# Paged-attention layer stack on one core: which bytes the values' trip through memory carries, and the order of stores, gathers and expert loads around it

## What is computed

```
x = x + einsum('bct,bcd->bdt', x, W0[cond])                        # layer 0: a 32x32 mix per sequence
x = x + x @ W^T + s * (x @ A[id]^T) @ Bm[id]^T                     # layer 1: dense plus a low-rank adapter
x = x + attention(x)                                               # layer 2
x = x + x @ W3[expert_id] + b3[expert_id]                          # layer 3: one 256x256 expert per sequence
```

## Time and profile before

| | us |
|---|---|
| median of 3 runs (155.38 to 156.30) | 156.03 |
| the profiled execution's own time | 154.9 |
| its span | 153.1 |
| busy: PE, DVE, ACT, POOL | 117.3, 88.8, 85.8, 62.0 |

### The profile page before, as it was taken

How to read it: one execution, slowest core, us unless ns; L and a number is a source line. 1 busy time by engine, 2 the same in 40 slices (tenths; PEclk the granted TensorE clock), 3 DMA queues, 4 the chain that set the end, 5 groups by cost and what they waited for, 6 DMA issues and landing times.

```text
span 153.1 us, 4138 instructions
## 1 busy us (share of the span) xinstructions
PE 117.3 (77%) x1418; PEld 91.0 (59%) x1418; DVE 88.8 (58%) x315; ACT 85.8 (56%) x236; POOL 62.0 (41%) x65
## 2 busy tenths in 40 slices
PE   7569599999989586076598392892599999999762
PEld 7559458998374163074466272672387787776631
DVE  0597988857528824860344003610867999989361
ACT  3119634698743629256589721472438878888200
POOL 7666779000008764787233300330333444734000
PEclk9999999999999977659969758699569999999999
DMA  3982999999963444799739998999976676766110
GB/s 94 244 249 62 370 424 407 423 405 374 395 173 100 132 119 114 247 313 392 315 110 269 422 355 210 401 377 279 253 232 205 197 242 204 222 207 180 37 39 34
DMA packets 29100, 37.60 MB, mean 246 GB/s; under 512 B 9497, under 2 KB 26781, under 8 KB 27438
## 3 DMA queue, kind: packets, MB, share of 16 engines
q1 hardware_dynamic: 26136, 23.98, 50.0%
q0 software_dynamic: 2528, 12.82, 22.2%
q10 hardware_dynamic: 416, 0.56, 1.2%
HBM read 31.39 MB, written 10.04 MB: 271 GB/s over the span
## 4 chain that ended last, share of the span: by engine, by line
DMA 42%; PE 20%; SPq 17%; issue 9%; POOL 5%; DVE 3%; ACT 2%; POOLq 1%; DVEq 0%
DMA kv_rows<-blkp 15%; DMA wr_rows<-blkp 11%; PE bank L1117 5%; DMA blkp<-wr_rows,patch_i 4%; PE bank L1063 4%; POOL wr_rows L500 4%; DMA blkp<-in_L_cond_W 4%; PE bank L1075 3%; PE bank L1128 3%; SPq L386 3%; DMA mask_rows<-span_m 3%; DMA scal<-in_L_cond_scalings 3%; SPq L364 2%; SPq L365 2%; SPq L348 2%
## 5 line engine op out<-in xcount | busy, mean ns | idle before, releaser
L520 POOL TENSOR_TENSOR xin_m<-xin_m,ri 128x704 f32<-128x704 f32 x15 | 21.8, 1454 | 44.4 <-DVE ri L924 44.4
L674 ACT ACTIVATE xin_m<-kvn_m,nb 128x176 f32<-128x176 f32 x64 | 27.6, 443 | 9.2 <-DVE nb L911 9.2
L911 DVE CUSTOM_DVE_ANT_0 kvn_m<-bank,mask_m 128x176 f32<-128x176 f32 x64 | 18.0, 336 | 14.6 <-PE bank L1063 11.0
L951 DVE TENSOR_TENSOR blkp<-blkp,cst 128x512 f32<-128x512 f32 x16 | 15.6, 1015 | 17.6 <-DMA blkp<-in_L_cond_W 17.6
L1063 PE MATMUL bank<-kt_m,natQ 32*64 32x176 f32 x256 | 15.7, 366 | 10.0 <-DVE nb L911 9.1
L1063 PEld LDWEIGHTS bank<-kt_m,natQ 32*64 32x64 f32 x256 | 9.5, 150 | 14.2 <-issue 13.1
L500 POOL DMA_INDIRECT wr_rows<-kvn_m,row_i x8 | 8.8, 1104 | 21.3 <-DMA wr_rows<-blkp 19.1
L684 ACT COPY x_m<-bank 128x512 f32<-128x512 f32 x16 | 9.4, 590 | 13.0 <-PE bank L1075 12.8
L1043 PE MATMUL bank<-cst,blkp 121*128 121x121 f32 (+1 forms) x48 | 9.0, 352 | 7.8 <-DMA blkp<-wr_rows,patch_i 7.8
L1043 PEld LDWEIGHTS bank<-cst,blkp 121*128 121x128 f32 (+1 forms) x48 | 7.3, 190 | 10.0 <-DMA blkp<-wr_rows,patch_i 9.0
L674 ACT ACTIVATION_READ_ACCUMULATOR xin_m<-kvn_m,nb 128x1 f32 x64 | 12.8, 200 | 0.0
(11 more groups left out here) (194 smaller groups left out, 257.4 us busy)
## 6 DMA issues: line engine op xcount, KB each, us to landing
blkp<-in_L_cond_W SPq DMA_DIRECT2D x32, 256.0 KB, 3.5
kv_rows<-blkp SPq DMA_DIRECT2D x3, 2048.0 KB, 10.3
wr_rows<-blkp SPq DMA_DIRECT2D x1, 1536.0 KB, 16.5
mask_m<-mask_rows SPq DMA_DIRECT2D x32, 44.0 KB, 5.4
vm_m<-kv_rows SPq DMA_DIRECT2D x4, 320.0 KB, 4.4
xin_m<-in_x SPq DMA_DIRECT2D x2, 512.0 KB, 5.6
out<-wq_m SPq DMA_DIRECT2D x8, 128.0 KB, 3.5
vm_m<-kv_rows SPq DMA_DIRECT2D x2, 384.0 KB, 4.6
```

Of the source, the lines that this page charges most:

```text
L520: pool.tensor_tensor(e_, e_, ri[:, p % 2, :].unsqueeze(2).broadcast_to([P, 4, KEYS]), ALU.mult).then_inc(s_pn, 1)
L674: act.activation(pr_seq(n % 2, u, j), S[:, n % 2, u, j, :], ACT.Exp, bias=nb[:, n % 2, 2 * u + j:2 * u + j + 1], scale=-1.0, accum_out=rs[ ...
L911: dve.tensor_tensor_reduce(S[:, n % 2, u, j, :], bank[2 + (2 * n + u) % 3][:, j * KEYS:(j + 1) * KEYS], mask[:, 2 * n + j, :], -SCALE, 3e3 ...
L951: tt(w_, w_, ident.unsqueeze(1).broadcast_to([P, B4, P]), ALU.add).then_inc(s_wx, 1)
```

## The change

1. SP: the 8 mask reads ahead of `wr_rows` out now come behind it. Masks 0 to 15 are read there; 16 to 19 behind values out 0, 20 to 23 behind values out 1, 24 to 31 behind values out 2. The loop waits for masks in groups of eight.
2. Values out sends only the v numbers and only the unit's own partitions (121, 121, 110 rows of 16 pieces of 512 bytes) to `v_rows`; the way back reads these.
3. SP's order is values out 0, back 0, experts 0 to 3, out 1, back 1, experts 4 to 7, out 2, back 2, experts 8 to 15. The latter now lie in `blkp[1]`.
4. POOL: patch 2 waits for values out 0. The bias gathers go into the pair loop, one a step at p = 2 to 9.
5. The copies (1,0), (1,1) and (2,1) go from ScalarE to VectorE, behind rotations(0).
6. q_part 2 and 3, but for their sums, go into the loop (n = 0 to 5), and turn_k 4 to 11 as well (two a step at n = 0 to 3; before, 4 and 5 lay ahead of the loop). ScalarE's zeroing of the v tails comes before x2 copies 2 and 3.

```diff
@@ -113,7 +114,7 @@
     with ctx:
         wr_rows = nc.dram_tensor("wr_rows", [ROWS, 2 * KV], F32).ap()
         wr_blocks = wr_rows.rearrange("(p o) c -> p (o c)", o=BLOCK)
-        kv_rows = nc.dram_tensor("kv_rows", [NU, P, BLOCK * 2 * KV], F32).ap()
+        v_rows = nc.dram_tensor("v_rows", [NU, P, BLOCK, KV], F32).ap()
         mask_rows = nc.dram_tensor("mask_rows", [P, KEYS + LAST], BF16).ap()
         cst = sb("cst", [P, cols.width])
...
@@ -196,8 +197,8 @@
         blkp = [sb(f"blkp{u}", [P, CH]) for u in range(NU)]
         by_o = [t[:, :].rearrange("p (o k c) -> p o k c", o=BLOCK, k=2) for t in blkp]
         blkw = blkp[2]
-        We = lambda b: blkp[(0, 2)[b % NE // 8]][:, (b % 8) * KC * D:(b % 8 + 1) * KC * D].rearrange("p (c o) -> p c o", c=KC)
-        We4 = lambda g: blkp[(0, 2)[g % B4 // 2]][:, g % 2 * B4 * KC * D:(g % 2 + 1) * B4 * KC * D] \
+        We = lambda b: blkp[b % NE // 8][:, (b % 8) * KC * D:(b % 8 + 1) * KC * D].rearrange("p (c o) -> p c o", c=KC)
+        We4 = lambda g: blkp[g % B4 // 2][:, g % 2 * B4 * KC * D:(g % 2 + 1) * B4 * KC * D] \
             .rearrange("p (b c o) -> p b c o", b=B4, c=KC)
         kt_m = sb("kt_m", [P, B * KEYS])
...
@@ -313,13 +315,16 @@
                 raw[i][0:n, :].rearrange("p (g o d) -> p g o d", g=G, o=BLOCK)
         MIX_DVE, MIX_ACT = ((0, 0), (0, 1), (0, 2), (1, 0), (1, 1)), ((0, 3), (1, 2), (1, 3))
-        KT_BANK = (3, 4, 0, 7, 3, 4, 7, 0, 7, 0, 7, 7)
-        KT_FREE = (0, 0, 0, 0, 1, 2, 4, 3, 7, 8, 9, 11)
+
+        KT_BANK = (3, 4, 0, 7, 0, 7, 0, 7, 7, 7, 7, 7)
+        KT_FREE = (0, 0, 0, 0, 3, 4, 5, 6, 8, 9, 10, 11)
         Q_BANK = (1, 2, 1, 2)
         QT_BANK = (5, 6)
-        QT_STEP = {1: 4, 2: 5, 3: 6, 4: 7}
-        KT_STEP = {0: (6, 7), 1: (8, 9), 2: (10,), 3: (11,)}
+        QT_STEP = {3: 4, 4: 5, 6: 6, 7: 7}
+        KT_STEP = {0: (4, 5), 1: (6, 7), 2: (8, 9), 3: (10, 11)}
+        Q_STEP = {0: (2, 1), 1: (2, 2), 2: (2, 3), 3: (3, 1), 4: (3, 2), 5: (3, 3)}
+        BIAS_STEP = 2
         L1_BANK = (5, 6)
...
@@ -362,15 +367,13 @@
             def load_mask(b):
                 x = sp.value_load(shift_i[0:1, b:b + 1], min_val=0, max_val=LAST)
-                sp.dma_start(mask[:, b, :], mask_rows[:, bass.ds(x, KEYS)]).then_inc(s_mask, 16)
-
-            for b in range(8):
-                load_mask(b)
+                sp.dma_start(mask[:, b, :], mask_rows[:, bass.ds(x, KEYS)]).then_inc(s_mask[b // MB], 16)
+
             for kv in range(2):
                 sp.wait_ge(s_perm[NU, kv], 1)
             sp.dma_start(wr_blocks, blkw[0:NWI, :]).then_inc(s_base, 16)
-            for b in range(8, B):
+            for b in range(2 * MB):
                 load_mask(b)
             sp.wait_ge(s_ids, 16)
...
@@ -378,7 +381,7 @@
                 if b < NE:
                     if b % 8 == 0:
-                        u = (0, 2)[b // 8]
+                        u = b // 8
                         sp.wait_ge(s_kt, 4 * (u + 1))
                         sp.wait_ge(s_vo[u], 16)
                 else:
...
@@ -390,7 +393,7 @@
             def values_out(u):
                 sp.wait_ge(s_patch[u], 16)
-                sp.dma_start(kv_rows[u], blkp[u][:, :]).then_inc(s_vo[u], 16)
+                sp.dma_start(v_rows[u, 0:PU[u]], by_o[u][0:PU[u], :, 1, :]).then_inc(s_vo[u], 16)
             def values_back(u):
                 sp.wait_ge(s_vo[u], 16)
...
@@ -399,7 +402,7 @@
                     for i in ((0, 0), (0, 1)):
                         sp.wait_ge(s_perm[i], 1)
                 b0, b1 = SEQS[0] * u, SEQS[0] * u + SEQS[u]
-                src = kv_rows[u][0:PU[u], :].rearrange("(b j) (o k c) -> (j o) b k c", j=WB, o=BLOCK, k=2)[:, :, 1, :]
+                src = v_rows[u, 0:PU[u]].rearrange("(b j) o c -> (j o) b c", j=WB)
                 for i in range(2):
                     b = b0 + (b0 + i) % 2
                     main, tail, lo = (KB, 0, KB) if i else (0, P, 0)
...
@@ -407,14 +410,20 @@
                     sp.dma_start(Vt[lo:lo + KB, b // 2:(b1 - 1 - i) // 2 + 1, i, :], src[tail:tail + KB, b - b0::2, :]).then_inc(s_v[u], 16)
             values_out(0)
+            for b in range(2 * MB, 2 * MB + 4):
+                load_mask(b)
             values_back(0)
-            values_out(1)
             for b in range(4):
                 expert(b)
+            values_out(1)
+            for b in range(2 * MB + 4, 3 * MB):
+                load_mask(b)
             values_back(1)
-            values_out(2)
             for b in range(4, 8):
                 expert(b)
+            values_out(2)
+            for b in range(3 * MB, B):
+                load_mask(b)
             values_back(2)
             for b in range(8, NE):
                 expert(b)
...
@@ -502,23 +511,31 @@
             pool.wait_ge(s_new, 16 * NT)
             pool.wait_ge(s_pidx, 1)
-            for u in range(NU):
+
+            def patch(u):
                 for kv in range(2):
                     pool.wait_ge(s_perm[u, kv], 1)
                 pool.indirect_dma_start(out=blkp[u][:, :], out_offset=None, in_=wr_blocks,
                                         in_offset=bass.IndirectOffsetOnAxis(ap=patch_i[:, u:u + 1], axis=0),
                                         bounds_check=NWI - 1, oob_is_err=False).then_inc(s_patch[u], 16)
+
+            patch(0)
+            patch(1)
+
+            pool.wait_ge(s_vo[0], 16)
+            patch(2)
             pool.wait_ge(s_eidi, 1)
             pool.wait_ge(s_l1, 4)
-            for n in range(NT):
-                pool.indirect_dma_start(out=be[n], out_offset=None, in_=b3,
-                                        in_offset=bass.IndirectOffsetOnAxis(ap=eid_i[:, n:n + 1], axis=0)).then_inc(s_be[n // 4], 16)
-
             for p in range(PAIRS - 1):
                 pool.wait_ge(s_ri, p + 1)
                 e_ = pr[:, p % 2, :, :].rearrange("p u r -> p (u r)").rearrange("p (i r) -> p i r", i=4)
                 pool.tensor_tensor(e_, e_, ri[:, p % 2, :].unsqueeze(2).broadcast_to([P, 4, KEYS]),
                                    ALU.mult).then_inc(s_pn, 1)
+                n = p - BIAS_STEP
+                if 0 <= n < NT:
+
+                    pool.indirect_dma_start(out=be[n], out_offset=None, in_=b3,
+                                            in_offset=bass.IndirectOffsetOnAxis(ap=eid_i[:, n:n + 1], axis=0)).then_inc(s_be[n], 16)
         @block.scalar
         def _(act):
...
@@ -630,38 +646,32 @@
             permute((0, 1))
             keep_k(1)
             root_k(1)
-            permute((1, 0))
             keep_v(1)
             act.wait_ge(s_woT, 1)
             act.copy(WoT[:, :, :], square(0)).then_inc(s_woTk, 1)
-            permute((1, 1))
             keep_x2(0)
             keep_x2(1)
             keep_qn(0)
             root_q(0)
             keep_qn(1)
             root_q(1)
-            permute((2, 1))
+
+            act.wait_ge(s_perm[2, 1], 1)
+            act.activation(vt_m[:, 0:RAW], ones[:, 0:1].broadcast_to([P, RAW]), ACT.Copy, scale=0.0).then_inc(s_vz, 1)
             keep_x2(2)
             keep_x2(3)
             keep_qn(2)
-
-            act.wait_ge(s_perm[2, 1], 1)
-            act.activation(vt_m[:, 0:RAW], ones[:, 0:1].broadcast_to([P, RAW]), ACT.Copy, scale=0.0).then_inc(s_vz, 1)
-            root_q(2)
             keep_qn(3)
-            root_q(3)
-            act.activation(warm[:, 1:2], eps[:, 0:1], ACT.Exp)
-            for c in range(6):
+            for c in range(4):
                 if c == 0:
                     act.wait_ge(s_perm[1, 0], 1)
                     act.wait_ge(s_perm[1, 1], 1)
                 keep_kt(c)
-                if c == 3:
-                    for t in range(2):
-                        keep_qt(t, bank[QT_BANK[0]][:, t * D:t * D + D])
-            for t in range(2):
-                keep_qt(2 + t, bank[QT_BANK[1]][:, t * D:t * D + D])
+            for t in range(4):
+                keep_qt(t, bank[QT_BANK[t // 2]][:, t % 2 * D:t % 2 * D + D])
...
@@ -892,17 +904,21 @@
             dve.wait_ge(s_eid, 1)
             cp(eid_i[:, :], eid[:, :]).then_inc(s_eidi, 1)
             rotations(0)
-            permute((2, 0))
+            for i in ((1, 0), (1, 1), (2, 0), (2, 1)):
+                permute(i)
             dve.wait_ge(s_rt, 8)
-            for i in range(4):
+            for i in range(2):
                 for piece in q_part[i]:
                     piece()
+            for i in range(2, 4):
+                q_part[i][0]()
             for n in range(PAIRS + RESULT):
                 if n < PAIRS:
                     if n == 0:
-                        dve.wait_ge(s_mask, 16 * B)
                         dve.wait_ge(s_new, 16 * NT)
+                    if n % (MB // 2) == 0:
+                        dve.wait_ge(s_mask[2 * n // MB], 16 * MB)
                     if n >= 2:
                         dve.wait_ge(s_exp, 4 * (n - 1))
                     dve.wait_ge(s_sc, n + 1)
...
@@ -942,6 +958,9 @@
                         dve.wait_ge(s_wo, g - 1)
```

(21 more changed lines are left out.)

23 lines of the change are left out of this document (12 added, 11 removed).

## The result

The changed kernel takes **166.74 us** (median of 3 runs, 164.59 to 167.39) against 156.03: a ratio of 1.063 [1.051, 1.076]. On another chip it was 163.01 against 156.21, 1.044 [1.037, 1.052]. So it is 4 to 6% slower; the intervals of the two ratios barely touch, and no run says why they differ. The forecast was 147.5, and no case of its range came. Every kernel has faster and slower executions: medians here are over all of them, ratios and their intervals over the faster ones alone. The profiled execution took 164.59, with a span of 162.8 (153.1 before).

A forecast was written before the change was run, and what follows sets the result against it. Up to about 108 us, data going to memory and back was taken to set the end. Span 153.1 - 9.4 + 1.0 = 144.7, own time 146.5, median 147.6, stated as 147.5; range 140.5 to 153.5.

The forecast's parts named there:

- part 5: SP's queue after out 0: experts 8 to 11 land at 104.2, third add stalls near 10 us, end 9.4 us sooner.
- part 3: Values out: half the bytes save about 1 us; out 0 takes 7.5 us (bounds 6.0 and 13.0), outs 1 and 2 10.3.
- parts 1 and 2: Store ahead of masks, then scatters: store issued at 25.5, landed at 33.5; patch 0 issued at 47.8, landed at 54.5.
- Masks 24 to 31 (8.3) lie under it, with 2 us to spare: SP's queue behind out 2: issuing these eight masks takes 8.3 us, hidden under the 10.3 us of the out.
- the estimate of 2.5 us for start and receipt: Store of the writers' blocks: 2.5 us added to 5.5 us of packets, so it lands at 33.5.
- the second half of the scatters now waits for the keys, not the store: POOL's scatters: keys, taken ready at 40.2, set the second half, so patch 0 is issued at 47.8.
- Part 6: The rest: q pieces, turns and exp table cost nothing; bias gathers in the pair loop add 1.0 us, bounds 0 and 2.
- A: Rival: outs use fewer DMA engines at full price, 1.8 us for each of three, 5.4 in all, 153.0; chance 0.15.
- C: Rival: the store is not let through, gains only 3.0 us; patch 0 goes out 7.5 later than forecast, 155.0; chance 0.08.
- D: Rival, slower: small pieces written from SBUF cost more than pieces read; at 100 ns a piece 24 us lost, 171; chance 0.07.
- B: Rival: small outs are cheap, 6.0 us for out 0 and 7.5 for out 1; 6.3 sooner, 141.2; chance 0.17.

The follow-up runs named there:

- a10: Changed kernel with masks 16 to 23 loaded with the first sixteen and 24 to 31 issued from ScalarE's queue; 158.46 us, 1.007 of the kernel before.
- a1: Changed kernel with values out sending all 128 partitions of a unit; 162.09 us, 1.039 of the kernel before.
- d1: Kernel before with only the new order, experts 0 to 3 ahead of out 1 and 4 to 7 ahead of out 2; 163.96 us, ratio 1.047.
- a4: Changed kernel, masks 16 to 23 with the first sixteen, 24 to 31 behind experts, outs ahead of experts again, 128 partitions out; 156.27 us, 0.989 of before.
- a8: a4 with experts 8 to 11 ahead of back 2, masks 24 to 31 on ScalarE's queue and whole 16 KB rows out; 154.39 us, 0.982 of before.
- a9: Changed kernel with values out sending whole 16 KB rows again, k and v; 162.65 us, 1.044 of the kernel before.

## Why the prediction was wrong

The place and the stall were forecast rightly: the third add waits for experts 8 to 11, which stand behind back 2. The time was not: 122.2 instead of 104.2. These 18.0 us are nearly the whole miss of the span (162.8 against 144.7); the median lies another 1.1 farther above the profiled execution than was carried over. **What failed are the terms of the chain up to that add**, 10.2 us of them in part 5, "SP's queue after that", with out 0 of part 3, and 7.8 in parts 1 and 2.

**The masks were called hidden.** "Masks 24 to 31 (8.3) lie under it, with 2 us to spare": they took 10.45 and started 2.2 us after the out, and back 2 came 12.7 us after out 2, not 10.3. In the first round the same: four masks 6.89 us, not 4.1. The 1.03 of the earlier trace rows is the price of the first eight masks alone. The same timeline of the kernel before has the price of the other 24, and it is 1.29 each:

```profile
29.65 30.97 SPq L365 DMA_DIRECT2D mask_m<-mask_rows  x24
```

By that row the eight masks take 10.3, all of out 2, and nothing is to spare; masks 0 to 15 took 1.29 each again. Taking the masks off the path is worth 4.6 us by medians (changed against a10, on two chips), and 4.4 at the third add. The cover of 2 us was no cover, with no bound on the term.

**Quiet prices in a chain.** Back 0 took 4.9 us to issue, not 2.1 (72.03 to 76.89). In a10, with no masks ahead of it, it took 2.1, and in a1, with masks but a store of 128 partitions, 2.5. So the excess seems to take both, the masks and the slower store. From there to the end of experts 0 to 3 it was 5.7, not 3.9: 0.9 passed before the first one was issued, which no term had, and the four took 4.78. Part 3's values out 0 took 9.7, over the 7.5 taken and within its bounds; without masks behind it, it was 8.7.

**The order was not priced.** This does not explain the 18.0 us, for the forecast had the new order's cost inside its 104.2. It explains why a slower kernel looked like a faster one. Part 5 followed the new chain and compared its end, 104.2, with the 113.6 of before. It never followed the old order through the same prices. From back 0 at 64.1: out 1 issued there lands at 74.4, with the 3.9 us of experts under it; back 1 76.5, out 2 landed 86.8, back 2 88.9, experts 8 to 11 issued by 92.8 and landed at 96.4. That is 7.8 us before 104.2, two times the 3.9 that the new order puts in series. d1 measured 7.2. So the forecast's own terms held the price of the worst part of the change, and it was never set apart, because the sum was made against the kernel before, and the new chain's end lay ahead of that kernel's third add. There the chain was hidden: the third add came 6.5 us after the second and waited 0.57. In the changed kernel it is the bound, and every us in it counts.

| step to the third add | forecast | measured | later by |
|---|---|---|---|
| patch 0 landed | 54.5 | 62.3 | 7.8 |
| out 0 to back 0 | 7.5 | 9.7 | 2.2 |
| back 0 issued | 2.1 | 4.9 | 2.8 |
| experts 0–3 | 3.9 | 5.7 | 1.8 |
| out 1 to back 1 | 10.3 | 9.6 | −0.7 |
| back 1 and experts 4–7 | 6.0 | 7.6 | 1.6 |
| out 2 to back 2 | 10.3 | 12.7 | 2.4 |
| the rest, to experts landed | 9.6 | 9.7 | 0.1 |

**Parts 1 and 2** are the largest single row. The packets' turns were right in kind: in 34 to 36 us of the changed kernel the two rings moved 40 and 36 packets, as in the earlier trace rows. But the store was issued at 28.58, not 25.5: ScalarE's copy of the writers' blocks ran from 26.59 instead of 23.56, after 5.3 us of waits on the unnamed queue. It landed 10.4 us after its issue, not 8.0, at 39.0 instead of 33.5. What was too small is the estimate of 2.5 us for start and receipt. SP's ring moved nothing until 32.0; then came 5 us of packets, near the 5.5 forecast, and 1.6 us more to the landing. In 28.5 to 31.5 us the gathers had the engines alone; this view has no row of q1:

```profile
q0 software_dynamic: 164, 1.21, 101.7%
```

So the step "the second half of the scatters now waits for the keys, not the store" failed: all eight stood behind the store, the first after 10.93 us of idle, at 39.83. Two of them took 2.33 and 1.97 us beside VectorE's copies, against 1.0. Patch 0 was issued at 54.95, not 47.8; had only the keys held it, which were ready at 42.2, it would be 49.8 by the forecast's terms. It landed 7.4 after its issue, not 6.7. Still the first scores came 6.6 us sooner; the forecast had 7.7.

**Part 3** said that half the bytes are worth about 1 us, not half. That held for 128 partitions (7.5 against 8.9, a4 and a8); with 121 and 110 the change got nothing for it (a9). **Part 6** is not contradicted: the tail from the third add, 40.6 against 39.5, is near the 1.0 that it had. No run takes the late norms, the turns or the bias gathers alone.

**The rivals.** A had the right mechanism: the row 66.0% is near 11 of 16 engines. By the rule in the Trainium skill (DMA: Bandwidth & Descriptors, Why a DMA increments its semaphore by 16 and not by 1) it would be 11, and the trace agrees. A's price in this order was about 1 us, though, since masks and not the store ended two of three outs. C's delay nearly came, 7.1 us at patch 0's issue where C had 7.5, but only in part by its mechanism: the store was let through, in 10.4 us instead of 16.5, only late. D did not hold: a packet of 31 ns is not a slow write. B is out. No case was "the masks and issues don't fit under the outs", which is what came, nor "the new order costs more than the rest brings"; these should have been D's place on the slower side.

## What to carry to other kernels

Where a queue issues transfers that wait for each other (out, then back), whatever is not needed at once belongs between the out and its back, never between a back and the next out, and only as much as fits by its contended price. To price a new order, follow both orders through the same terms; the difference of the ends is the order's price, whatever the rest of the change brings. Where the sum itself says that a chain of issues becomes the next bound, each of its terms needs an upper bound from the busiest row, not the quietest.
